# Side buffer of a two-attention kernel split in two banks, and row maxima taken for two heads at a time from high halves

## What is computed

```python
h = _layernorm(x) * (1 + ca) + sa
x = x + ga * _L0_attn_ref(h, ...)     # one head of width 128, no mask
h = _layernorm(x) * (1 + cb) + sb
x = x + gb * _L0_ffn_ref(h, ...)      # h + attention(rmsnorm(h)), then experts
...
# the second attention: 4 key heads, 4 query heads on each, width 64, rotary, causal
scores = jnp.einsum('btghk,bThk->bghtT', qg, k)
scores = jnp.where(mask, scores, -jnp.inf) / np.float32(np.sqrt(K))
p = jax.nn.softmax(scores, axis=-1)
```

## Time and profile before

| | |
|---|---|
| median of three runs | 1379.15 us (1377.59 to 1379.6) |
| profiled execution, its own time | 1377.09 us |
| its span | 1375.3 us |
| first `scoresB` starts | 299.6 us into the span |
| last exp of the second attention | 1156.6 us |
| mean granted TensorE clock | 0.921 |

### The profile page before, as it was taken

One profiled execution on the slowest core, in us unless ns is written; L12 is line 12 of the kernel. 1 busy time (PEld: TensorE's weight loads), 2 busy tenths in 40 slices (PEclk: granted clock), 3 DMA queues, 4 the chain that ended last, 5 costly groups with the idle time before them and its releaser, 6 DMA issues.

```text
span 1375.3 us, 35916 instructions
## 1 busy us (share of the span) xinstructions
PE 1123.1 (82%) x14984; PEld 841.2 (61%) x14984; DVE 1056.3 (77%) x2097; ACT 840.2 (61%) x1488; POOL 1000.7 (73%) x786
## 2 busy tenths in 40 slices
PE   4767776459999999999999999999999998610891
PEld 2666666126667676776676766767767676510781
DVE  5576665768889889888898898888988975583665
ACT  2644555258778787787787777877877886100230
POOL 2554567659888888898898888988988897317355
PEclk9999998579999999999999999999999999555896
DMA  6140001122122121122221211212212110013694
GB/s 210 41 142 1 1 2 68 41 88 52 54 67 49 50 74 37 51 59 55 59 52 46 74 36 54 57 55 58 52 47 48 36 26 1 1 35 116 193 301 153
DMA packets 49246, 90.84 MB, mean 66 GB/s; under 512 B 8896, under 2 KB 19136, under 8 KB 48832
## 3 DMA queue, kind: packets, MB, share of 16 engines
q1 hardware_dynamic: 46128, 81.21, 20.7%
q0 software_dynamic: 2960, 7.38, 1.9%
HBM read 43.96 MB, written 13.01 MB: 41 GB/s over the span
## 4 chain that ended last, share of the span: by engine, by line
PE 64%; DVE 19%; POOL 6%; issue 5%; SPq 3%; ACT 2%; DMA 1%; POOLq 0%; DVEq 0%
PE psT L1082 5%; PE psS L1152 5%; PE psS L1151 5%; PE psT L1070 5%; PE psS L1173 5%; PE psS L1174 5%; PE psS L1175 4%; PE psT L1100 3%; PE psO L1082 3%; PE psO L1152 3%; PE psO L1151 3%; POOL rows_in L708 2%; DVE pmax L1552 2%; DVE nmax L1401 2%; DVE psT L1529 2%
## 5 line engine op out<-in xcount | busy, mean ns | idle before, releaser
L682 POOL TENSOR_TENSOR probs<-arena,probs 128x512 f16<-128x512 f32 x576 | 652.3, 1157 | 113.5 <-ACT probs L866 113.1
L866 ACT ACTIVATE probs<-arena 128x512 f16<-128x512 f32 x576 | 358.0, 622 | 0.0
L874 ACT ACTIVATE arena<-psS 128x512 f32<-128x512 f32 x384 | 228.1, 594 | 144.7 <-PE psS L1155 82.4
L1173 PE MATMUL psS<-vb,probs 128*128 128x65 f16 x2304 | 301.9, 192 | 4.6 <-POOL probs L682 2.4
L1174 PE MATMUL psS<-vb,probs 128*128 128x64 f16 x2304 | 303.3, 194 | 0.0
L1175 PE MATMUL psS<-vb,probs 128*128 128x65 f16 x2304 | 301.4, 192 | 0.0
L1173 PEld LDWEIGHTS psS<-vb,probs 128*128 128x128 f16 x2304 | 220.0, 97 | 72.7 <-issue 9.4
L1174 PEld LDWEIGHTS psS<-vb,probs 128*128 128x128 f16 x2304 | 215.4, 97 | 47.4
L1552 DVE TENSOR_REDUCE pmax<-psT 128x1 f32<-128x512 f32 (+1 forms) x305 | 193.6, 639 | 39.7 <-PE psT L1082 19.0
L1175 PEld LDWEIGHTS psS<-vb,probs 128*128 128x128 f16 x2304 | 216.8, 98 | 0.0
L1152 PE MATMUL psS<-arena 65*128 65x512 f16 (+1 forms) x448 | 157.1, 351 | 0.0
(11 more groups left out here) (268 smaller groups left out, 2884.6 us busy)
## 6 DMA issues: line engine op xcount, KB each, us to landing
arena<-arena SPq DMA_DIRECT2D x240, 128.0 KB, 2.4
arena<-w_exp_dram SPq DMA_DIRECT2D x40, 384.0 KB, 4.2
arena<-xnT_d SPq DMA_DIRECT2D x16, 512.0 KB, 3.8
wkv<-w_d SPq DMA_DIRECT2D x16, 352.0 KB, 4.2
rows_in<-arena POOLq DMA_DIRECT2D x1, 2580.0 KB, 18.6
arena<-rows_in SPq DMA_DIRECT2D x40, 64.5 KB, 3.1
arena<-x_dram SPq DMA_DIRECT2D x4, 512.0 KB, 5.3
hres<-x_dram SPq DMA_DIRECT2D x4, 512.0 KB, 5.0
```

The lines of the kernel that those rows point to most:

```text
L682: pool.tensor_tensor(pl[:, r, :], pf[:, r, :], ph[:, r, :], ALU.subtract).then_inc(lo_P, 1)
L866: act.activation(ph[:, s % RING, :], pf[:, s % RING, :], ACT.Copy).then_inc(b_hi, 1)
L874: act.activation(pf[:, s % RING, :], score_banks[s % SCORES], ACT.Exp).then_inc(b_exp, 1)
L1173: pe.matmul(dst, high, vb[:, p, j, 0:OW], start=first, stop=False, skip_group_check=True)
```

## The change

In the first attention the side buffer becomes two banks with a task each: every part, projection and maximum is split in halves of 512 columns or assigned to bank 0, PE waits only for the last task of that bank, DVE reduces each half and then the two halves' maxima to one. On PE and ACT the parts move behind `scoresA(t)` and exp. In the second attention "max" entries come in pairs, two heads at once, one from partitions 0 to 63 (qB, kB) and one from partitions 64 to 127 (qA, kC), high halves alone; the side work is laid out anew, with high and low halves taken at other steps, a counter of its own for the low queries of the first pair, and the prologue makes the maxima of two heads, and half of those of the next two.

```diff
-EARLY = {4: (0,), 5: (1,), 6: (2,), 7: (3,), 8: (4, 5)}
-LATE = {0: (6,), 1: (7,), 2: (8,), 3: (9,)}
-ROW_AT = 5
+THIS_PAIR = {2: 5, 5: 6, 7: 7, 9: 8, 11: 9}
+NEXT_PAIR = {14: 0, 16: 1, 17: 2, 19: 3, 20: 4, 22: 5, 24: 6, 26: 7, 28: 8, 29: 9}
+LATER_PAIR = {31: 0, 32: 1, 33: 2, 34: 3, 35: 4}
+ROWS_AT = {13: 2, 15: 3, 31: 4, 33: 5}
...
-PROJ = {0: ("k", 0), 1: ("k", 1), 3: ("q", 0, 0), 5: ("r", 0, 0), 7: ("q", 0, 1), 9: ("r", 0, 1), 11: ("v",),
-        13: ("q", 1, 0), 15: ("r", 1, 0), 17: ("q", 1, 1), 19: ("r", 1, 1)}
-OUTP = {21: ("turn", 0), 23: ("turn", 1), 25: ("turn", 2), 27: ("turn", 3), 30: ("out", 0), 33: ("out", 1)}
-HIGH_AT = {4: 0, 12: 1, 22: 2}
-LOW_AT = {5: 0, 15: 1, 25: 2}
+PROJ = {0: ("k", 0), 1: ("k", 1), 3: ("q", 0, 0), 4: ("r", 0, 0), 6: ("q", 0, 1), 7: ("r", 0, 1), 9: ("v",),
+        16: ("q", 1, 0), 18: ("r", 1, 0), 21: ("q", 1, 1), 24: ("r", 1, 1)}
+OUTP = {11: ("turn", 0), 13: ("turn", 1), 15: ("turn", 2), 17: ("turn", 3), 20: ("out", 0), 23: ("out", 1)}
+HIGH_AT = {4: 0, 10: 1, 26: 2}
+LOW_AT = {5: 0, 11: 1, 27: 2}
...
-PROLOGUE = ([PROJ[s] for s in sorted(PROJ)] + [("max", G, n) for n in range(len(PIECES))] + [("row", G)]
-            + [("max", G + 1, n) for c in sorted(EARLY) for n in EARLY[c]])
+PROLOGUE = ([PROJ[s] for s in sorted(PROJ)] + [e for n in range(len(PIECES)) for e in pair(G, n)]
+            + [("row", G), ("row", G + 1)] + [e for s in sorted(LATER_PAIR) for e in pair(G + 2, LATER_PAIR[s])])
...
             for t in range(NL):
                 first, after = side_of(t)
+                scoresA(t)
                 for e in first:
                     side_task(SIDE_AT[e])
-                scoresA(t)
...
+            def fill_pair(e, banks, p, n):
+                g = e[1] % G
+                if g == 0 and e[2] == 0:
+                    pe.wait_ge(qk_in, 112 * n + 112)
+                if g == 2 and e[2] == 0:
+                    pe.wait_ge(q1_in, 96 * n + 96)
+                w = min(4, PIECES[e[2]][0][0] + 1 - 4 * PIECES[e[2]][0][1]) * P
+                for k, (i, h) in enumerate(PIECES[e[2]]):
+                    diag = h == i // 4
+                    mm = [pe.matmul(banks[0][:, k * w:(k + 1) * w], qB[0:HD, p, g, i * P:(i + 1) * P],
+                                    kB[0:HD, p, h * 512:h * 512 + w], start=True, stop=not diag),
+                          pe.matmul(banks[1][:, k * w:(k + 1) * w], qA[HD:P, p, g + 1, i * P:(i + 1) * P],
+                                    kC[HD:P, p, h * 512:h * 512 + w], start=True, stop=not diag)]
+                    if diag:
+                        mm = [pe.matmul(dst[:, (k + 1) * w - P:(k + 1) * w], identh[:, :], maskh[:, :],
+                                        start=False, stop=True) for dst in banks]
...
             def row_max(t):
-                v.wait_ge(a_side, SIDE_END["max", t])
-                v.tensor_reduce(nmax[:, t % 4:t % 4 + 1], psTf, AX.X, ALU.max, negate=True).then_inc(a_top, 1)
+                for h in range(2):
+                    v.wait_ge(a_side, SIDE_END["max", t, h])
+                    v.tensor_reduce(halfmax[:, t % 4, h:h + 1], psT[:, h, :], AX.X, ALU.max).then_inc(a_top, 1)
+                v.wait_ge(a_top, 2 * t + 2)
+                v.tensor_reduce(nmax[:, t % 4:t % 4 + 1], halfmax[:, t % 4, :], AX.X, ALU.max, negate=True).then_inc(a_neg, 1)
```

More of the change, by code:

```diff
@@ L88, in side_work @@
     for s in range(SPR):
-        h, c = divmod(s, SPH)
         now = []
[L91 to L94, removed]
+        if s in THIS_PAIR:
+            now += pair(2, THIS_PAIR[s])
+        if not last and s in NEXT_PAIR:
+            now += pair(G, NEXT_PAIR[s])
+        if not last and s in LATER_PAIR:
+            now += pair(G + 2, LATER_PAIR[s])
         if not last and s in PROJ:
@@ L98, in side_work @@
             now.append(OUTP[s])
-        if c == ROW_AT and not (last and h == G - 1):
-            now.append(("row", h + 1))
+        if s in ROWS_AT and not (last and ROWS_AT[s] >= G):
+            now.append(("row", ROWS_AT[s]))
         steps.append(now)
@@ L144, in side_of @@
     b, i = divmod(t, NT)
-    first = [("part", b + 1, i - 3)] if 3 <= i < 7 and b + 1 < B else []
+    first = [("part", b + 1, i - 3, h) for h in range(2)] if 3 <= i < 7 and b + 1 < B else []
     if i == 7:
@@ L482, in _ @@
             store_input2(2)
-            spread_row(start(0, "A"), 0, 0)
+            spread_row(1, 0, 0)
+            spread_row(2, 0, 1)
             store_input2(3)
@@ L808, in _ @@
                 act.activation(pf0[:, r, :], psS[:, t % 2, :], ACT.Exp, scale=A_SCALE).then_inc(a_E, 1)
+                if 3 <= i < 7 and b + 1 < B:
+                    for h in range(2):
+                        part_high(b + 1, i - 3, h)
                 act.wait_ge(a_E, t + 1)
@@ L1031, in _ @@
             side_task(0)
+            side_task(1)
             mod_of(2)
@@ L1034, in _ @@
             pe.wait_ge(wq_lo, 2)
-            for n in range(1, len(FIRST_SIDE)):
+            for n in range(2, len(FIRST_SIDE)):
                 side_task(n)
@@ L1123, in side @@
                 e = entries[i]
-                if e[0] == "gap":
+                if e[0] == "gap" or e[0] == "max" and e[1] % 2 == 1:
                     return
@@ L1129, in side @@
                 prev = e[0] in ("turn", "out")
+                if e[0] == "max":
+                    before(entries, i + 1, base, prior)
+                    fill_pair(e, [side_banks[bank], side_banks[(i + 1) % SB]], (1 - p) if nxt else p, it + 1 if nxt else it)
+                    return
                 if prev:
```

147 lines of the change are left out of this document (73 added, 74 removed).

## The result

The changed kernel takes 1523.1 us (median of 4 runs, 1521.7 to 1524.3) against 1378.4 for the kernel before (median of 4, 1375.9 to 1379.6): ratio 1.105, 95% interval 1.103 to 1.107. Slower was right, 1405 and the range up to 1450 were not.

| stretch | before | after | difference | predicted |
|---|---|---|---|---|
| to the last exp of the first attention | 227.9 | 198.1 | -29.8 | -33 |
| from there to the first exp of the second | 72.3 | 87.0 | +14.7 | +8 |
| fifteen rounds | 815.4 | 974.0 | +158.5 | +51 |
| last round | 41.0 | 39.3 | -1.7 | 0 |
| from the last exp to the end | 218.6 | 221.5 | +2.9 | 0 |

A forecast was written before the change was run, and what follows sets the result against it. PE was taken to bound the second attention's rounds. 1377.1 - 33 (first attention) + 8 (prologue) + 51 (fifteen rounds) = 1403, and 2.1 more for the median: 1405 us, range 1340 to 1450.

The forecast's parts named there:

- First attention: Split side buffer and parts behind the scores make tiles, projections and first parts shorter: -33 us in all.
- the parts ahead of it: The four parts ahead of tile 0 in the first attention overlap by halves: 4 us gained.
- The other terms: First attention: input-turning tiles gain 5 us, projections 9, scores not waiting for gate work 4; added DVE reductions cost 3.
- Prologue: Between the attentions, twenty maxima instead of ten and more ahead of the first scores: +8 us, between +4 and +10.
- the maxima of the next heads: Prologue: ten instead of six stand ahead of the second attention's first scores, the last of them alone: +2.4 us.
- (a): Second pair's low halves land late for step 31 of each round with a next one: PE stands 5.3 us.
- (b): First pair's high halves, taken at step 10 and used at step 14: PE waits 1.5 us a round.
- (c): PE waits for DVE: 1.0 us at step 3 and about 1.0 in sum at steps 11 to 20.
- The 58.0: Forecast length in us of each of 15 second-attention rounds, against 54.6 before: +3.4 a round, +51 in all.
- The pairs' term: Two heads' maxima run at once on half the array's rows each, halving 7.7 us: -3.8 us of PE a round.
- rival 3: Round's 48 changes of array mode cost at most 8 us: 1510 us, a third 1440; chance 0.10 including no pairing.
- Rival 2: Clock falls to half behind each round's long stall: 15 x 2 = +30, 1435 us; chance 0.17.

The follow-up runs named there:

- order_full: Changed kernel's order, but each head's maxima from all 128 rows, unpaired, the first pair also waiting for its low halves: 1604.5 us.
- one_half_high: high_wait with both heads of a pair on partitions 0 to 63, so they run one after the other: 1515.0 us.
- high_wait: Changed kernel, but the second pair's maxima wait for high halves only, its low halves getting their own counter: 1458.4 us, ratio 1.060.
- before_64: Kernel before, with maxima made from high halves on 64 rows, one head at a time, unpaired, in the old order: 1518.7 us.
- grouped: high_wait with the two pairs of a two-block piece adjacent and their masks behind both: 1451.8 us, ratio 1.054.
- one_half: Changed kernel with both heads of a pair on partitions 0 to 63, so they can't run at once: 1648.6 us.

## Why the prediction was wrong, point by point

1. **First attention, right in sum.** -33 forecast, -29.8 in the changed kernel and -28 alone. Part tiles take 5.4 us where 5.1 was worked out, so nine of them give 12.6 of the 14; the first tile's exp starts at 38.33 us instead of 41.26, 2.9 of the 4 for the parts ahead of it. The other terms weren't measured apart. (The stated terms of a part tile, 3.1 and 1.5, make 4.6; 5.1 needs the 0.43 of the maxima's scores, which the tile still has.)
2. **Prologue, half of it missed.** +8 forecast, +14.7 measured. The step took twenty maxima at the 0.56 us apiece of the earlier trace rows. That pace holds while PE fills one bank as DVE reads another. A pair takes two banks of three, so the next pair needs one of this pair's banks, and PE can begin it only when DVE has read that one. The changed kernel's PE in the prologue, then DVE's first maximum and the row's, then ACT's norm2_out(3):

```profile
256.89 0.58 PE L1119 MATMUL psT<-arena 64*128 64x512 f16 x1 [6.78 <-DVE pmax L1591]
...
258.60 0.58 PE L1119 MATMUL psT<-arena 64*128 64x512 f16 x1 [0.77 <-DVE pmax L1591]
...
260.06 0.48 PE L1119 MATMUL psO<-arena 64*128 64x384 f16 x1 [0.85 <-DVE pmax L1591]
...
256.06 0.68 DVE L1591 TENSOR_REDUCE pmax<-psO 128x1 f32<-128x512 f32 x1
...
271.32 0.17 DVE L1611 TENSOR_REDUCE hmax<-pmax 128x8 f32<-128x16 f32 x1
...
272.89 2.43 ACT L767 ACTIVATE arena<-hres,rstd2b 128x128 f32<-128x128 f32 x8
```

   A pair comes every 1.5 to 1.7 us, PE and DVE in turn, at clock 0.50 for PE: 20 maxima take 15.3 us (first maximum 256.06, row's maximum 271.32) where 11.2 were forecast. That is 4.1 of the missing 6.7; order_full, with full-height maxima in the same order, takes as long (16.1). A second row to turn puts another 0.7 ahead of norm2_out(3), and from there to the first exp it is 12.2 us (272.89 to 285.1) instead of 7.9 (292.33 to 300.2), +4.3 where +2.4 was forecast for the maxima of the next heads, again because they come in pairs, one each 1.5 us or so.
3. **Stalls, right.** (a) 4.8 for 5.3, (b) 1.7 for 1.5, (c) 2.2 for 2.0. In (c) the sum came out by luck in part: 1.0 was forecast for the keys at step 3 and step 2 has 0.4; 1.0 was forecast for steps 11 to 20, and steps 16 and 20 have 0.7 and 0.4; the 0.6 at step 34 wasn't foreseen. Together 8.7 us a round for the 8.8 forecast. The 58.0 was 49.3 of work and 8.8 of waits, rounded.
4. **The pairs' term failed.** The step "I take -3.8, since nothing in the rows makes them share anything but the array" priced the change of mode at nothing, and put it in rival 3 with a share of 0.10. Pairing itself is worth 3.4 us of PE (one_half_high against high_wait). The 48 changes cost 0.09 to 0.10 us each, 4.3 to 5.0 us (one_half_high less the order's 0.5, before_64). With the order's 0.5, and 3.4 off for the pairs, that makes +1.4 to +2.1 us where the table shows +1.2 (54.5 against 53.3); the difference is what such sums are good for. Instead of -3.8 it is +1.2: 5.0 us a round, **75 us** of the miss. Rival 3's own bound, 8 us for 48, held; its "a third of it" was too low and its full price too high. (For "all 8" its sum adds 7 us a round, without a reason.) The Trainium skill ("TensorEngine Tiling (Array Packing)", Key Properties) says that a change of tiling mode drains TensorE; the gaps of 0.1 us agree with that.
5. **Rival 2 came true beside it.** The clock falls behind each stall, 3.4 us at 0.50, as the earlier trace rows let fear. It costs 3.9 / 2 = 1.9 us a round, **29 us**, beside the 30 of rival 2 (which took 6 us at half clock and hid 1 of the loss); the forecast priced it but as a separate case. 75 + 29 = 104 of the 107 us that the rounds lacked.

Rivals 2 and 3 were set against the forecast as alternatives, though neither excludes the other nor the forecast. As both are mechanisms that add, the slow end of the range should have been their sum: 1405 + 30 + 35 is 1470 with rival 3 at a third, and more with the whole.

## What to carry to other kernels

Half-height matmuls in a stream of full-height ones pay about 0.10 us at each change, 0.2 for an excursion. By these numbers (an estimate) two 512-column products run side by side save 0.21 us and just earn it back, and anything narrower loses, so collect them in runs (grouped) or leave them at full height. Let a wait count only the transfers that its user reads; one counter for two kinds of halves made a stall of 4.8 us, of which about 1 us is left without it. And where a stall on PE is foreseen, add the half clock behind it to its price, and add rivals that can come true together.

## What the runs showed that had not been expected

- The change between 64 and 128 rows costs about 0.10 us each way on PE. Unpaired half-height matmuls show it in PE's work (0.10 from 96 changes a round, 0.09 to 0.10 from 48); paired ones show it in the starts (0.32 us where 0.21 is the rule) and in grouped, where 8 changes fewer take 0.6 us away, 0.08 each. A change between 65 and 128 rows costs nothing that shows (0.21 and 0.16 us between starts at 512 and 384 columns).
- A short stall can cost far more clock than its own length. Stalls of 4.3 us a round left PE at 1.2 GHz for 17.9 busy us a round in one_half, though it was busy without a break behind them; in the changed kernel, with a stall of 4.8 us, it was 3.9 busy us. With the stall gone it was 4.4 and 0.9 us, and even then a wait of 1.7 us stood ahead of 17.1 us at half clock. What decides how long it lasts wasn't found.
- Pairs run side by side start within 0.01 us of one another, and save 3.4 of the 3.8 us of PE a round that half the columns' time would be.
